# GpSimd writes a pair's probability tails ahead of the main part, and the tails' transposes wait for a count of their own

## The reference, cut to what matters

```python
def reference(x, ctx_1024, mask, Wq, bq, Wk, bk, Wv, bv, Wo, bo, norm_g, norm_b, slot_g, ...):
    # cross attention: x is (2, 1024, 256), the context (2, 154, 256), 16 heads of 64
    q = (layernorm(x) @ Wq + bq) ; k = (ctx @ Wk + bk) ; v = (ctx @ Wv + bv)   # by heads
    s0 = jnp.einsum('bhqd,bhkd->bhqk', q, k) / math.sqrt(D_HEAD)
    p = jax.nn.softmax(jnp.where(mask_mat, NEG, s0), axis=-1)    # 154 keys a row
    s1 = jnp.einsum('bhqk,bhkd->bhqd', p, v)
    x = x + s1.reshape(b, sq, D_MID) @ Wo + bo
    # then a soft mixture of 16 experts with 64 slots each
    logits = jnp.einsum('bnd,esd->bnes', layernorm(x), se)
    dispatch, combine = softmax over tokens, softmax over slots
    ...
    return x + jnp.einsum('bns,bso->bno', combine, eout)
```

## Time and profile before

| what | us |
|---|---|
| runs shown | 552.88, 552.14, 552.45 |
| median | 552.45 |
| span of the profiled execution, first to last instruction | 550.3 |
| TensorE busy in that span | 533.1 (97%) |
| weight loads busy | 499.6 (91%) |
| VectorE busy | 432.9 (79%) |
| ScalarE busy | 403.1 (73%) |
| GpSimd busy | 310.1 (56%) |

### The profile page before, as it was taken

One profiled execution on the slowest core, in us unless ns is written; L12 is line 12 of the kernel. 1 busy time (PEld: TensorE's weight loads), 2 busy tenths in 40 slices (PEclk: granted clock), 3 DMA queues, 4 the chain that ended last, 5 costly groups with the idle time before them and its releaser, 6 DMA issues.

```text
span 550.3 us, 11967 instructions
## 1 busy us (share of the span) xinstructions
PE 533.1 (97%) x3896; PEld 499.6 (91%) x3896; DVE 432.9 (79%) x1301; ACT 403.1 (73%) x1098; POOL 310.1 (56%) x331
## 2 busy tenths in 40 slices
PE   7999999999999999999998999999999999989997
PEld 4889999999999999999997888999988877889997
DVE  6787878787897979899668998898698688755553
ACT  5879969596896959689564546689978888656562
POOL 6665654534544455454366768885569999910000
PEclk9999999999999999999999999999999999999999
DMA  8635000000020000000001343150288887515651
GB/s 257 185 77 174 3 1 2 2 2 1 9 90 2 2 2 0 4 0 4 0 1 79 152 186 140 61 198 25 82 273 273 268 301 246 179 55 186 181 164 68
DMA packets 34901, 54.11 MB, mean 98 GB/s; under 512 B 3997, under 2 KB 21497, under 8 KB 34713
## 3 DMA queue, kind: packets, MB, share of 16 engines
q1 hardware_dynamic: 34841, 53.36, 29.3%
HBM read 40.54 MB, written 10.49 MB: 93 GB/s over the span
## 4 chain that ended last, share of the span: by engine, by line
PE 69%; POOL 18%; ACT 4%; DVE 3%; issue 3%; SPq 2%; DMA 2%; POOLq 0%; DVEq 0%; ACTq 0%
PE ps L1577 8%; PE ps L1352 8%; PE ps L1364 8%; PE ps L1544 7%; PE ps L1456 7%; POOL w_gu_low L785 7%; PE ps L1491 6%; PE ps L1434 5%; POOL wkq_low L785 5%; PE ps L1468 4%; PE ps L1493 3%; PE ps L1636 2%; PE ps L1602 2%; POOL prob L721 2%; DMA wvo_raw<-in_L_xattn_Wo_dram 2%
## 5 line engine op out<-in xcount | busy, mean ns | idle before, releaser
L721 POOL TENSOR_TENSOR prob<-expo,prec 128x512 f32<-128x512 f32 x64 | 66.7, 1043 | 93.2 <-DVE prec L1143 92.0
L882 ACT ACTIVATE expo<-expo,nmin 128x154 f32<-128x154 f32 x256 | 106.2, 423 | 5.3 <-DVE nmin L1132 4.8
L1132 DVE CUSTOM_DVE_ANT_0 expo<-ps,maskb 128x154 f32<-128x154 f32 x256 | 69.0, 312 | 11.9 <-PE ps L1456 11.7
L1152 DVE TENSOR_TENSOR pT_low<-ps,pT_high 128x512 fp32r<-128x512 f32 (+1 forms) x96 | 57.3, 597 | 5.9 <-ACT pT_high L896 5.5
L1456 PE MATMUL ps<-kbd,qT_high 128*128 128x308 f32 x256 | 61.1, 323 | 0.0
L896 ACT CAST pT_high<-ps 128x512 fp32r<-128x512 f32 (+1 forms) x96 | 49.2, 514 | 13.5 <-PE ps L1468 9.1
L785 POOL TENSOR_TENSOR w_gu_low<-w_raw,w_gu_high 128x1024 fp32r<-128x1024 f32 x17 | 50.8, 2990 | 13.8 <-ACT w_gu_high L832 13.8
L800 ACT ACTIVATE oT_high<-ps,bqv_c 128x256 fp32r<-128x256 f32 x64 | 29.9, 467 | 34.7 <-PE ps L1493 34.7
L882 ACT ACTIVATION_READ_ACCUMULATOR expo<-expo,nmin 128x1 f32 x256 | 50.3, 197 | 0.0
L1040 DVE TENSOR_TENSOR w_gu_low<-w_raw,w_gu_high 128x1024 fp32r<-128x1024 f32 x14 | 35.3, 2518 | 8.9 <-ACT w_gu_high L832 8.8
L1456 PEld LDWEIGHTS ps<-kbd,qT_high 128*128 128x128 f32 x256 | 39.8, 190 | 0.2
(11 more groups left out here) (240 smaller groups left out, 1733.1 us busy)
## 6 DMA issues: line engine op xcount, KB each, us to landing
logits_dram<-lsb SPq DMA_DIRECT2D x16, 512.0 KB, 2.6
w_raw<-in_L_ffn_Wg_dram SPq DMA_DIRECT2D x16, 512.0 KB, 3.7
w_raw<-in_L_ffn_Wu_dram SPq DMA_DIRECT2D x16, 512.0 KB, 4.5
w_raw<-in_L_ffn_Wd_dram SPq DMA_DIRECT2D x16, 512.0 KB, 4.7
lraw<-logits_dram SPq DMA_DIRECT2D x13, 512.0 KB, 3.8
out_dram<-gate SPq DMA_DIRECT2D x16, 128.0 KB, 2.2
kbd<-keys SPq DMA_DIRECT2D x12, 154.0 KB, 2.8
wvo_raw<-in_L_xattn_Wv_dram SPq DMA_DIRECT2D x2, 512.0 KB, 6.9
```

Of the source, the lines that this page charges most:

```text
L721: pool.tensor_tensor(prob[:, n % 2, :, heads, :], expo[:, n % 2, pp, :, :, 0:P], prec[:, n % 2, pp].unsqueeze(3).to_broadcast([P, 2, 2, P] ...
L882: ins = act.activation(row, row, ACT.Exp, scale=-1.0, bias=nmin[:, n % 2, pp, j, h:h + 1], accum_out=psums[:, n % 2, pp, j, h:h + 1])
L1132: ins = dve.tensor_tensor_reduce(out=expo[:, n % 2, pp, j, h, :], in0=ps[:, s % NS, h * SK:(h + 1) * SK], in1=maskb[:, (2 * (n // QUADS) + ...
L1152: dve.tensor_tensor(pT[1][0:rows, n % 2, 2 * t:2 * t + tiles], ps[0:rows, NS + k % NT, 0:tiles * 2 * P].rearrange("p (t n) -> p t n", t=ti ...
```

## The change

On GpSimd the two instructions of an R event change places: the tail (`prob_t`) is written first and raises a new count, `tail_ready`; the main part follows and raises `norm_ready`. On TensorE T2, which reads the tails alone, waits for `tail_ready` in place of `norm_ready`. T0 and T1 wait for the same `norm_ready` numbers as before. VectorE's waits for `norm_ready` (L1127 and L1142, where a buffer of `expo` and `prec` is used again) stay as they are, and now mean the end of the main part.

```diff
-    recip_ready, norm_ready = sem("recip_ready"), sem("norm_ready")
+    recip_ready, norm_ready, tail_ready = sem("recip_ready"), sem("norm_ready"), sem("tail_ready")
...
                 heads = slice(2 * pp, 2 * pp + 2)
-                pool.tensor_tensor(prob[:, n % 2, :, heads, :], expo[:, n % 2, pp, :, :, 0:P],
-                                   prec[:, n % 2, pp].unsqueeze(3).to_broadcast([P, 2, 2, P]), ALU.mult)
                 pool.tensor_tensor(prob_t[:, n % 2, :, heads, :], expo[:, n % 2, pp, :, :, P:SK],
                                    prec[:, n % 2, pp].unsqueeze(3).to_broadcast([P, 2, 2, TAIL]), ALU.mult)\
+                    .then_inc(tail_ready, 1)
+                pool.tensor_tensor(prob[:, n % 2, :, heads, :], expo[:, n % 2, pp, :, :, 0:P],
+                                   prec[:, n % 2, pp].unsqueeze(3).to_broadcast([P, 2, 2, P]), ALU.mult)\
                     .then_inc(norm_ready, 1)
...
                     pe.wait_ge(t_free, k - NT + 1)
-                pe.wait_ge(norm_ready, 2 * n + 1 + (t > 0))
+                if t < 2:
+                    pe.wait_ge(norm_ready, 2 * n + 1 + t)
+                else:
+                    pe.wait_ge(tail_ready, 2 * n + 2)
```

## The result

| kernel | median, us | runs, us |
|---|---|---|
| before, beside the changed kernel | 552.58 | 552.14 to 552.88 |
| changed | 548.95 | 548.39 to 549.34 |

The ratio is 0.9935, with an interval of 0.9923 to 0.9947. The change gains 3.6 us; 3.6 was forecast, and the median lies 0.1 us from the predicted 548.85. The interval means a gain of 2.9 to 4.3 us, so an agreement within 0.1 us is closer than these runs can tell.

The account below looks back on a forecast made before the run. TensorE was taken as the bound, with time to win where T2 waits for GpSimd's tail. Terms 2.00 + 0.19 + 0.56 + 0.63 + 0.04 + 0.15 = 3.57 us gave 548.85 us, range 548.2 to 550.4.

Parts of the forecast that it names:

- The five small waits: Five more steps where T2's load starts within 0.12 us of the tail's end, no idle listed: 0.15 us in all.
- the 206 us step: Fifth norm chain: of 0.50 us won, only 0.19 kept, because GpSimd's slot instructions and R0 hold T0.
- the ordinary steps: Steps where T0 has 0.34 us of room; pairs 0.5 us longer would lose 0.16 in some 13, 2.1 us.
- T1 clears by 0.06: Behind the first chain, the main part, now written last, releases T1's load at 77.59 us; it is due at 77.65.
- chain 6: Norm chain near 239 us: T1's load, held by the main part, could start at 238.75 instead of 239.31; 0.56 us kept.
- first four chains: Norm chains near 78, 110, 142 and 174 us: T2's wait disappears, 0.50 us each, 2.00 together.
- Chain 7: Norm chain near 271 us: T2's load 0.67 us late, less 0.04 that T1 catches up; 0.63 kept.
- The eighth: T2's wait at 277.5 us: nearly nothing gained, as the last step's R0 hangs on ScalarE's row; 0.04 us kept.
- main part takes the tail's place: Rival at T1: TensorE would stand there as long as it stood at T2, no gain, 552.4 us; chance 0.07.
- A part of it is given back: Rival: longer pairs or collisions use up T1's room; 550.4 us, between 549.6 and 551.2; chance 0.12.
- Slower: Rival: GpSimd's pair markedly longer in the new order, every later R pays; 554.4 us; chance 0.04.
- The collisions: VectorE instructions reading two SBUF tiles holding up GpSimd's pair: up to 0.48 us each, none new expected.

Follow-up runs that it names:

- the kernel with the 57 other pairs: Against the kernel before, the change on all R pairs except the seven directly behind a norm chain: 552.24 us, 0.9997.
- the kernel with the seven pairs: Against the kernel before, the change only on R1 of steps 5, 9, ... 29, directly behind a norm chain: 549.34 us, 0.9948.
- The experiment: Changed kernel plus one tiny GpSimd instruction between tail and main part in all 64 pairs: 549.40 us, 0.9943 against before.
- this run: Changed kernel plus three tiny GpSimd instructions between tail and main part in all 64 pairs: 552.02 us, 1.0001 against before.
- the moved chain: Kernel before, without the change, with GpSimd's seven norm instructions behind the next R0 in the first seven groups: 549.88 us, 0.9962.

## Why the prediction was right, point by point

The mechanism was right, and the large terms of the sum were right in size. The five small waits were not, and of the rival cases the 206 us step and the ordinary steps were mis-sized.

*What bounds the kernel, and the unit.* Right. One wait was put at 0.50 us; the first four gave 1.93, 0.48 each. The comparison with an undisturbed step gave it. The listed idle would have given the same where nothing behind it was short of room (0.49 for 0.48 to 0.50, and at 271 us 0.62 for 0.63), but in T2 of step 30 an idle of 0.53 was worth 0.1.

*The swap costs nothing.* Shown. The pair takes 0.32 + 1.05 = 1.37 us, forecast at 1.36 to 1.40. The swap alone and the count alone are at 0.9998 and 0.9999.

*T1 clears by 0.06.* Shown at 78.25 us; behind chain 6 the room is gone, as forecast, and T1's load (237.19) starts 0.11 behind the end of the main part (236.04 + 1.04).

*The sum.* Against the table: first four chains 2.00, measured 1.93. The 206 us step 0.19, measured 0.24 (1.93 to 2.17). Chain 6 0.56, measured 0.61 (2.17 to 2.78). Chain 7 0.63, measured 0.63. The eighth 0.04, measured 0.10: it wins 0.49 at T1 and gives 0.45 back at T0 of step 31. The five small waits, put at 0.15, gave next to nothing. One of them (T2 of step 4, 64.98 us) lies ahead of the stretch. The other four (213, 220, 246 and 252 us) are gone in the kernel with the 57 other pairs, which gains 0.02 us from T1 behind chain 5 to T1 of step 28; and the kernel with the seven pairs, which leaves them as they were, has the same 2.2 us at T1 of step 24 as the change. That term stood on rows in which no idle was listed, and half of an invisible wait was too much. Sum 3.57, measured 3.51: the 0.07 too much at the first four chains and the 0.15 here are nearly made good by 0.05 to 0.06 too little at each of the 206 us step, chain 6 and the eighth, so the closeness of the sum is in part luck.

*Who takes back the gain at 206 us.* GpSimd's slot instructions, as the step said, but moving them only moves the wait (0.34 at the next Q), since VectorE then waits for the slot result. I had not seen this second limit behind the first.

*What comes after.* From T1 of step 31 to the end it takes 265.6 us after and 265.4 before, so the 3.5 are carried through to within 0.2. The first load of the logits comes at 289.43 us in place of 292.35; with the 0.59 of the late start that is 3.5.

*The rival "main part takes the tail's place"* fell; so did the doubt that the change acts.

*"A part of it is given back"* was priced at 0.7 us for 0.12 us more in each pair. The experiment has 0.63 for 0.15: the size came out, but by parts that missed both ways, which is luck. The first four chains give back almost nothing (0.03, where 0.06 each was forecast), and the 206 us step with its chain gives back 0.30 in place of 0.06 + 0.13 = 0.19, since both of its pairs delay T0 by their full 0.15.

*"Slower"* was mis-sized. I let it decide from about 0.3 us a pair; 0.43 us gives the time of before and not more. The term that failed is T0 of the ordinary steps, 2.1 us at 0.5 us a pair and 1.3 in the expectation of this run: T0 has 0.34 of room, but what it loses beyond that is made up within the same step. Of the 0.38 expected at T1 behind a chain, 0.36 came and 0.30 lasted.

*The collisions* did not come in the changed kernel, as said: the main parts take 1.04 to 1.05 us in the chain steps. They do exist, as the moved chain shows, at 0.16 and 0.25 us each, within the 0.48 that I took as the bound.

## What to carry to other kernels

When one engine writes two results for another under one count, ask which result is read first and whether the writer is ever late; where it is late, the one read first should be written first with a count of its own, and only the late occurrences pay (here seven of 64). Cost a wait by the distance to a matmul that does not wait in a step without it, and then look for the next release behind it, since the room there (here 0.06 us) says how sure the gain is. A wait at an engine that many others feed may have a second limit close behind: moving GpSimd's slot instructions removed one wait of 0.27 and made one of 0.34.

## What the runs showed of the hardware beyond that

The steady part repeats far better than the whole. T1 of step 4 to T1 of step 31 took 219.37, 219.44 and 219.46 us in three kernels that should be alike (before, the swap alone, the count alone), and 215.83 and 215.86 in two executions of the change. But T1 of step 4 started anywhere from 64.81 to 66.64 us in the thirteen profiled executions. In before and after, 0.58 of the 0.59 us between them is there already when ScalarE gets `Wo`, for whose transfer it stands idle in both. The kernel before is first:

```profile
51.82 1.06 ACT L810 ACTIVATE wvo_high<-wvo_raw 128x1024 fp32r<-128x1024 f32 x1 [0.95 <-DMA wvo_raw<-in_L_xattn_Wo_dram]
```
```profile
52.40 1.06 ACT L811 ACTIVATE wvo_high<-wvo_raw 128x1024 fp32r<-128x1024 f32 x1 [1.21 <-DMA wvo_raw<-in_L_xattn_Wo_dram]
```

So a difference of a few tenths of a us is better read from a stretch than from medians.

A GpSimd instruction in a row costs less than its duration. The tiny one is listed at 194 ns and moves the next one by 0.15 us; three of them move it by 0.43.
